# Contexts in sets of one quad, and one-bank pieces in a ring of four for the maximum pass

## The chip, the cores and the metric

The kernel runs on one core of one Trainium2 chip. The metric is the device time of one execution in microseconds (us). Five engines work side by side, each through its own list of instructions in order: TensorE (PE, matrix products), VectorE (DVE), ScalarE (ACT), GpSimd (POOL), and SyncE (SP), which here issues most of the DMAs. They wait for each other through semaphores. PE writes its results to PSUM, eight banks of 128 partitions by 512 fp32 columns; DVE and ACT read them from there.

## The reference

Two layers on 2048 tokens of width 128. Layer 0 is a Mamba block and then an attention block with a mixture of 16 experts; layer 1 is a second attention block and a mixture of 8 experts. The change touches only the two attention blocks. Each computes, for one sequence of 2048 tokens and 16 heads of width 8, in short:

```python
q, k, v = split(q), split(k), split(v)
...
scores = jnp.einsum("bhqd,bhkd->bhqk", q, k)
scores = jnp.where(causal, scores, neg)
attn = jax.nn.softmax(scores, axis=-1)
ctx = jnp.einsum("bhqk,bhkd->bhqd", attn, v)
...
```

The softmax needs the exact maximum of each query's row of scores before the exponentials are taken.

## The kernel before

Each head makes its scores twice. Queries and keys are cut into 16 tiles of 128 and four chunks of 512.

**The maximum pass** (`ring_piece` on PE, `ring_read` on DVE). PE multiplies a tile of 128 queries by up to 512 keys into `psum_b` (L840), DVE reduces the result to one maximum for each query (L1038 with the causal mask, which is a custom instruction followed by a short read of its accumulator; L1041 without a mask). The products are grouped into pieces by `MAX_PIECES`. Before the change a piece fills two banks (up to 1024 columns), there are 19 of them for a head, and `psum_b` is a ring of `NB = 2` such pieces: PE may start piece n when DVE has released piece n - 2. A head has 40 products in this pass and 24 reads. When the last piece of a head has been read, DVE runs five short instructions (L1046 to L1050), which split the negated maxima in three bf16 parts; PE transposes them (L844, the "maxrow", itself a ring piece), DVE copies them out (L1052), and SP sends them through memory into the rows of the queries' operand, so that the second pass gives scores with the maximum taken off.

**The second pass** (`scores`, `exp_piece`). PE makes the scores again, now keys by queries, into three banks of `psum_a` used in turn (L852; a diagonal block gets a product with the mask behind it, L855). ACT takes the exponential (L980) into a tile in SBUF. A head has 36 such steps ("slots"): for chunk c of the queries three for the diagonal quad of blocks and four for each full quad before it, c of them. Scores run three slots ahead of the slot in hand (`LOOK = 3`).

**The contexts** (`context`, `read_context`). For each quad, four fp32 products with 32 stationary columns each, in four column groups of the array, add to the fourth bank of `psum_a` (L870). The trace records each of the four as two. `SETS` says which quads go together: six sets for a head, four of them of two quads and two of one. A set stands in PE's order behind the scores of the slot in which its last quad's exponentials are awaited. When the last set of a chunk is done, ACT copies the bank out (L971). There is only one context bank, so the first set of the next chunk, the one with its diagonal quad, waits for that copy.

**The order.** `step_order` writes out what PE issues for a head: for each of the 36 slots the scores, then ring pieces until the DVE time they stand for has caught up with the slot, then a context set. `AHEAD_MAX` pieces of the head after the next are already made in this head, the rest of the next head's first. Heads go in pairs: once a pair, in its first head, PE also sums the two heads' contexts (L878, read by DVE at L1058) and transposes them (L885, read at L1063 and L1066); both use ring pieces. Before the first head stands a prologue (`FIRST_RING`) with the maxima alone, 29 pieces before the change. The last pair has no head behind it: its first head has only the rest of the last head's maxima to make, its second head none.

Of the kernel before, what the change touches and what calls it, by code (L numbers as in the profile page):

```python
# [12 lines left out]
P = 128  # L13
# [3 lines left out]
CW = 512  # L17
NC = T // CW
# [19 lines left out]
def program(nc, a, out):  # L38

    with ExitStack() as ctx:  # L40
# [10 lines left out]
        extra = sb("extra", [P, 4112])  # L51
        psum_a = ctx.enter_context(nc.psum_tensor("psum_a", [P, T], F32))
        psum_b = ctx.enter_context(nc.psum_tensor("psum_b", [P, T], F32))
# [485 lines left out]
        for c in range(NC):  # L539
            for ks in ((0,), (1,), (2, 3)):  # L540
                SCORES.append((c, [(4 * c + k, k, CW - k * P, (k - ks[0]) * 2 * P) for k in ks], "diagonal", c))
            for f in range(c):
# [5 lines left out]

        SETS = [(0, [("diagonal", 0)]), (1, [("diagonal", 1), ("full", 0)]), (2, [("diagonal", 2), ("full", 1)]), (2, [("full", 2)]),
                (3, [("diagonal", 3), ("full", 3)]), (3, [("full", 4), ("full", 5)])]  # L550
        NS_H = len(SETS)
        SET_OF = {q: n for n, (_, quads) in enumerate(SETS) for q in quads}
# [5 lines left out]
        def tail(i):  # L558
            return (i % 4 + 1) * P
        MAX_PIECES = [([(0, 0, P, 0), (2, 0, 3 * P, P), (3, 0, CW, CW)], [(0, 0, 0, P, True), (2, 0, P, 3 * P, True), (3, 0, CW, CW, True)]),  # L560
                      ([(1, 0, 2 * P, 0), (9, 2, 2 * P, 2 * P), (11, 2, CW, CW)],
                       [(1, 0, 0, 2 * P, True), (9, 1, 2 * P, 2 * P, True), (11, 1, CW, CW, True)]),
                      ([(8, 2, P, 0), (10, 2, 3 * P, P)], [(8, 1, 0, P, True), (10, 1, P, 3 * P, True)])]
        MAX_PIECES += [([(i, 0, CW, 0), (i, 1, tail(i), CW)], [(i, 0, 0, CW + tail(i), True)]) for i in range(4, 8)]
        MAX_PIECES += [([(i, 0, CW, 0), (i, 1, CW, CW)], [(i, 0, 0, 2 * CW, False)]) for i in range(8, 16)]
        MAX_PIECES += [([(i, 2, CW, 0), (i, 3, tail(i), CW)], [(i, 1, 0, CW + tail(i), True)]) for i in range(12, 16)]
        NB = 2
        NMAX = len(MAX_PIECES)
        AHEAD_MAX = 9
        SUM_SLOT, TURN_SLOT = 8, 14  # L570
# [71 lines left out]
        def attention(L, x_in, norm, w_cols, wt_raw):  # L642
            s = Attention()
# [42 lines left out]
            s.unread = extra[:, 1024:2048].bitcast(BF16).rearrange("p (b n) -> p b n", b=NB)  # L686
            s.mpart = extra[:, 2048:2080].rearrange("p (t c) -> p t c", c=2)
            s.mneg = extra[:, 2112:2128]
# [10 lines left out]
        def ring(n):  # L699
            return psum_b[:, (n % NB) * 2 * CW:(n % NB + 1) * 2 * CW]  # L700
        context_bank = psum_a[:, 3 * CW:4 * CW]
# [1017 lines left out]
```

How the kernel before makes its waits and increments, by code:

```python
        def turn_normed(e, name, xn, filled):  # L114
            for c in range(NC):
                e.wait_ge(tile_normed, normed(name) - NC + c + 1)
                for t in range(4 * c, 4 * c + 4):
                    i = e.transpose(psum_a[:, t * P:(t + 1) * P], xn[:, t * P:(t + 1) * P], ident[:, :])
                i.then_inc(filled, 1)
# [1 line left out]
        def read_turned(e, xT, filled, read):  # L122
            for c in range(NC):
                e.wait_ge(filled, c + 1)
                e.activation(xT[:, c * CW:(c + 1) * CW], psum_a[:, c * CW:(c + 1) * CW], ACT.Copy).then_inc(read, 1)
# [3 lines left out]
        def dve_link(e, ins):  # L130
            counts["dve"] += 1
            ins.then_inc(dve_step, 1)
            e.wait_ge(dve_step, counts["dve"])
# [1 line left out]
        def act_link(e, ins):  # L135
            counts["act"] += 1
            ins.then_inc(act_step, 1)
            e.wait_ge(act_step, counts["act"])
# [1 line left out]
        def pool_link(e, ins):  # L140
            counts["pool"] += 1
            ins.then_inc(pool_step, 1)
            e.wait_ge(pool_step, counts["pool"])
# [1 line left out]
        def norm_dve(e, name, src, dst, affine=None):  # L145
# [4 lines left out]
                    e.bn_stats(stats[:, bass.ds(4 * c + k, 1), :].rearrange("p a b -> p (a b)"),  # L150
                               src[:, ds(4 * c + k, D)]).then_inc(tile_stats, 1)
            e.wait_ge(tile_stats, NT * (n + 1))
            for t in range(NT):
# [127 lines left out]
        def mamba_pool(e):  # L281
            e.wait_ge(consts_ready, CONSTS)
            e.memset(xm[:, :, 0:3], 0.0).then_inc(xm_padded, 1)
```

## Time and profile before

| | |
|---|---|
| median of 3 runs | 2043.42 us (2042.29 to 2044.32) |
| profiled execution | 2041.5 us, span 2039.8 us |
| PE busy | 1564.7 us (77% of the span) |
| DVE busy | 1237.7 us (61%) |
| ACT busy | 875.0 us (43%) |
| first attention, first maximum product to last context | about 470 to 988 us |
| second attention | about 1277 to 1800 us |

The profile page gives busy time for each engine and the costliest groups of instructions. A busy PE is not a PE at its peak, since the ends of matmuls are modelled; starts are measured, so the distance from one start to the next is what counts for PE. The granted clock of PE is shown in tenths of full speed; 0.5 is its lower level.

### The profile page before, as it was taken

How to read it: one execution, taken by the hardware profiler on the slowest of the kernel's cores; microseconds unless marked ns; L12 is line 12 of the kernel's file. 1: busy time of each engine (PE TensorE's matmuls, PEld its weight loads, DVE VectorE, ACT ScalarE, POOL GpSimd, SP SyncE). 2: the span in 40 equal slices, each digit the busy share in tenths (PEclk: the TensorE clock that was granted, in tenths of full speed). 3: DMA queues.
4: the chain of work that ended last, by engine and by line, in shares of the span. 5: the costliest groups of instructions: out<-in, count | busy, mean ns of one | idle time of the engine just before them, and what ended most of it. 6: DMA issues, size and time to landing. Idle time of an engine off the chain costs nothing.

```text
span 2039.8 us, 27036 instructions
## 1 busy us (share of the span) xinstructions
PE 1564.7 (77%) x8103; PEld 671.6 (33%) x8104; DVE 1237.7 (61%) x2336; ACT 875.0 (43%) x1663; POOL 411.2 (20%) x267
## 2 busy tenths in 40 slices
PE   4817756636999999999524912799999999868999
PEld 2302222321333333332213802233333333235665
DVE  2479999476777777774240115777777777324444
ACT  2353323010766667666301301166666666631111
POOL 4019989110000011010123061001001110000000
PEclk9958889965999999998757956599999999968999
DMA  2002213013111111110141122211111110000000
GB/s 69 6 29 81 82 62 114 0 51 91 36 37 48 34 37 47 36 35 13 52 132 49 50 49 93 49 37 36 48 36 35 47 45 26 13 16 8 23 15 29
DMA packets 59071, 91.76 MB, mean 45 GB/s; under 512 B 13001, under 2 KB 39057, under 8 KB 58993
## 3 DMA queue, kind: packets, MB, share of 16 engines
q1 hardware_dynamic: 56962, 86.79, 14.7%
q0 software_dynamic: 2048, 4.20, 0.9%
q8 instruction: 33, 0.54, 0.1%
q14 instruction: 28, 0.23, 0.0%
HBM read 74.63 MB, written 16.32 MB: 45 GB/s over the span
## 4 chain that ended last, share of the span: by engine, by line
PE 59%; DVE 23%; issue 6%; ACT 5%; POOL 3%; DMA 2%; DVEq 1%; SPq 1%; POOLq 0%; ACTq 0%
PE psum_a L870 16%; PE psum_b L840 11%; PE psum_a L852 9%; DVE arena L516 5%; DVE extra L1038 5%; DVE arena L490 3%; PE psum_a L1509 3%; PE psum_b L1509 3%; PE psum_b L326 2%; DVE extra L1041 2%; PE psum_a L326 2%; PE psum_b L1518 2%; ACT psum_a L432 2%; PE psum_a L1518 1%; POOL expert_inputs L1259 1%
## 5 line engine op out<-in xcount | busy, mean ns | idle before, releaser
L980 ACT ACTIVATE arena<-psum_a 128x512 f32<-128x512 f32 (+3 forms) x1280 | 585.6, 546 | 254.5 <-PE psum_a L852 152.5
L1038 DVE CUSTOM_DVE_ANT_0 extra<-psum_b,mask_q 128x128 bf16<-128x128 f32 (+7 forms) x512 | 365.4, 755 | 200.5 <-PE psum_b L840 200.2
L840 PE MATMUL psum_b<-arena 72*128 72x512 bf16 (+3 forms) x1280 | 362.3, 372 | 94.1 <-DMA arena<-k_parts 50.8
L852 PE MATMUL psum_a<-arena 75*128 75x512 bf16 (+3 forms) x1280 | 395.2, 357 | 11.4 <-ACT arena L980 4.5
L1041 DVE TENSOR_REDUCE extra<-psum_b 128x1 f32<-128x1024 f32 x256 | 300.6, 1219 | 64.0 <-PE psum_b L840 62.6
L870 PE MATMUL psum_a<-arena,extra 128*32 128x512 f32 x2560 | 336.6, 637 | 2.2 <-ACT arena L980 2.2
L852 PEld LDWEIGHTS psum_a<-arena 75*128 75x128 bf16 x1280 | 118.3, 98 | 337.9 <-ACT arena L980 156.7
L295 POOL TENSOR_TENSOR arena<-arena,extra 128x1024 f32<-128x1024 f32 x48 | 170.9, 3574 | 130.0 <-DVE arena L516 118.0
L840 PEld LDWEIGHTS psum_b<-arena 72*128 72x128 bf16 x1280 | 102.0, 100 | 241.4 <-DVE extra L1038 108.1
L786 POOL TENSOR_TENSOR arena<-arena 128x512 f32<-128x512 f32 x64 | 81.1, 1268 | 465.1 <-ACT arena L971 310.5
L971 ACT ACTIVATE arena<-psum_a 128x512 f32<-128x512 f32 x128 | 76.4, 597 | 137.5 <-PE psum_a L870 137.5
L364 PE MATMUL psum_b<-arena,ident 128*128 128x512 f32 x192 | 104.1, 675 | 16.3 <-DVE arena L500 11.0
L870 PEld LDWEIGHTS psum_a<-arena,extra 128*32 128x32 f32 x2560 | 66.0, 112 | 135.4 <-issue 116.4
L774 POOL COPY extra<-arena 128x128 f32 (+1 forms) x32 | 9.5, 301 | 491.7 <-PE psum_a L870 491.7
L855 PE MATMUL psum_a<-mask_k,ident_bf 128*128 128x128 bf16 x512 | 100.2, 223 | 0.0
L354 PE MATMUL psum_a<-arena,select 96*128 96x512 bf16 x64 | 21.8, 425 | 98.0 <-DVE arena L490 93.3
L432 ACT ACTIVATE psum_a<-arena,a_neg 128x1024 f32<-128x1024 f32 x32 | 35.8, 1117 | 117.8 <-DVE arena L516 112.1
L490 DVE TENSOR_TENSOR arena<-arena,psum_a 128x2048 f32<-128x2048 f32 x32 | 72.4, 2263 | 1.5 <-PE psum_a L354 1.5
L1509 PE MATMUL psum_a<-arena 128*128 128x512 f32 x144 | 66.3, 604 | 6.8 <-DVE arena L1598 6.8
L174 ACT ACTIVATE spread<-spread 128x16 f32<-128x16 f32 x6 | 1.3, 216 | 149.7 <-DVE spread L156 149.7
L1509 PE MATMUL psum_b<-arena 128*128 128x512 f32 x144 | 64.8, 592 | 0.0
L1058 DVE COPY arena<-psum_b 128x512 f32<-128x512 f32 x16 | 11.1, 692 | 84.7 <-PE psum_b L878 83.0
(263 smaller groups left out, 1707.8 us busy)
## 6 DMA issues: line engine op xcount, KB each, us to landing
arena<-q_parts SPq DMA_DIRECT2D x192, 96.0 KB
arena<-k_parts SPq DMA_DIRECT2D x192, 96.0 KB
extra<-c_rows SPq DMA_DIRECT2D x32, 512.0 KB, 3.6
arena<-in_L_ffn_fc_w_dram SPq DMA_DIRECT2D x32, 256.0 KB, 5.9
k_parts<-arena SPq DMA_DIRECT2D x10, 512.0 KB, 5.6
q_parts<-arena SPq DMA_DIRECT2D x6, 512.0 KB, 5.0
arena<-in_L_ffn_w_dram SPq DMA_DIRECT2D x24, 128.0 KB, 2.1
expert_inputs<-zeros SPq DMA_DIRECT2D x4, 512.0 KB, 6.0
```

The costliest lines, as they stand in the source:

```text
L295: e.tensor_tensor(hc[step % 2][m], hs[step % 2][:, m, :], c_rows[step % NCB], ALU.mult).then_inc((hc0_done, hc1_done)[m], 1)
L364: i = e.matmul(psum_b[:, m * HALF + c * CW:m * HALF + (c + 1) * CW], ident[:, :], hc[step % 2][m][:, c * CW:(c + 1) * CW], start=(step % N ...
L490: e.tensor_tensor(dBu[step % 2], du[:, :, h * HALF:(h + 1) * HALF], psum_a[:, 0:HALF].unsqueeze(1).to_broadcast([P, NM, HALF]), ALU.mult). ...
L516: e.tensor_tensor_scan(hs[step % 2][:, m, :], (dA0, dA1[step % 2])[m], dBu[step % 2][:, m, :], start, ALU.mult, ALU.add).then_inc(scan_don ...
L840: m = e.matmul(ps[:, at:at + width], s.mq[0:ROWS, b, i * P:(i + 1) * P], s.mk[0:ROWS, b, c * CW:c * CW + width], start=True, stop=True)
L852: m = e.matmul(score_bank(p)[:, at:at + width], s.ek[0:ROWS + 3, b, j * P:(j + 1) * P], s.eq[0:ROWS + 3, b, (c + 1) * CW - width:(c + 1) * ...
L855: m = e.matmul(score_bank(p)[:, at:at + P], ident_bf[:, :], mask_k[:, :], start=False, stop=True)
L870: m = e.matmul(context_bank[32 * k:32 * k + 32, :], s.vs[:, b, j, :], probabilities(s, b, kind, quad, k, CW), start=(kind == "diagonal"), ...
L980: m = e.activation(probabilities(s, b, kind, quad, k, width), score_bank(p)[:, at:at + width], ACT.Exp)
L1038: m = e.tensor_tensor_reduce(s.unread[:, n % NB, at:at + length], ps[:, at:at + length], mask_q[:, 2 * CW - length:], 1.0, NEG, ALU.add, A ...
L1041: m = e.tensor_reduce(s.mpart[:, i, c:c + 1], ps[:, at:at + length], AX.X, ALU.max)
L1509: i = e.matmul(ps[:, (KH * m + k) * CW:(KH * m + k + 1) * CW], w[:, b, k * P:(k + 1) * P], xfT[:, c * CW:(c + 1) * CW], start=True, stop=True)
```

## The change

`SETS` becomes one set for each quad, ten for a head. Ring pieces become one bank wide: `max_piece` packs narrow products to 512 columns, a head has 34 pieces, `NB` is 4, so that PE may start piece n when piece n - 4 is released, and `AHEAD_MAX` is 17. The products of the maximum pass and their columns stay the same (40 products, 17408 columns for a head); the reads on DVE go from 24 to 40, 16 of them masked as before. `mpart` gets four columns for each tile in place of two. The rest follows from `step_order`.

```diff
--- before.py
+++ after.py
@@ -546,8 +546,9 @@
         LOOK = 3
         assert NSC % LOOK == 0
 
-        SETS = [(0, [("diagonal", 0)]), (1, [("diagonal", 1), ("full", 0)]), (2, [("diagonal", 2), ("full", 1)]), (2, [("full", 2)]),
-                (3, [("diagonal", 3), ("full", 3)]), (3, [("full", 4), ("full", 5)])]
+        SETS = []
+        for c in range(NC):
+            SETS += [(c, [("diagonal", c)])] + [(c, [("full", c * (c - 1) // 2 + f)]) for f in range(c)]
         NS_H = len(SETS)
         SET_OF = {q: n for n, (_, quads) in enumerate(SETS) for q in quads}
         SET_END = [max(p for p, x in enumerate(SCORES) if x[2:] in quads) for _, quads in SETS]
@@ -557,16 +558,21 @@
 
         def tail(i):
             return (i % 4 + 1) * P
-        MAX_PIECES = [([(0, 0, P, 0), (2, 0, 3 * P, P), (3, 0, CW, CW)], [(0, 0, 0, P, True), (2, 0, P, 3 * P, True), (3, 0, CW, CW, True)]),
-                      ([(1, 0, 2 * P, 0), (9, 2, 2 * P, 2 * P), (11, 2, CW, CW)],
-                       [(1, 0, 0, 2 * P, True), (9, 1, 2 * P, 2 * P, True), (11, 1, CW, CW, True)]),
-                      ([(8, 2, P, 0), (10, 2, 3 * P, P)], [(8, 1, 0, P, True), (10, 1, P, 3 * P, True)])]
-        MAX_PIECES += [([(i, 0, CW, 0), (i, 1, tail(i), CW)], [(i, 0, 0, CW + tail(i), True)]) for i in range(4, 8)]
-        MAX_PIECES += [([(i, 0, CW, 0), (i, 1, CW, CW)], [(i, 0, 0, 2 * CW, False)]) for i in range(8, 16)]
-        MAX_PIECES += [([(i, 2, CW, 0), (i, 3, tail(i), CW)], [(i, 1, 0, CW + tail(i), True)]) for i in range(12, 16)]
-        NB = 2
+        def max_piece(*reads):
+            at, products, taken = 0, [], []
+            for i, c in reads:
+                width = CW if c < i // 4 else tail(i)
+                products.append((i, c, width, at))
+                taken.append((i, c, at, width, c == i // 4))
+                at += width
+            return products, taken
+        MAX_PIECES = [max_piece((1, 0), (5, 1)), max_piece((9, 2), (13, 3))]
+        for g in range(NC):
+            MAX_PIECES += [max_piece((4 * g, g), (4 * g + 2, g)), max_piece((4 * g + 3, g))]
+            MAX_PIECES += [max_piece((i, c)) for i in range(4 * g, 4 * g + 4) for c in range(g)]
+        NB = 4
         NMAX = len(MAX_PIECES)
-        AHEAD_MAX = 9
+        AHEAD_MAX = 17
         SUM_SLOT, TURN_SLOT = 8, 14
 
         def step_order(first=False, turns=False, maxima=True, early=True, scores=True):
@@ -684,7 +690,7 @@
             s.oe_sum = slot(2).rearrange("p (c n) -> p c n", c=NC)
             s.sum_turned = slot(3)[:, 0:CW]
             s.unread = extra[:, 1024:2048].bitcast(BF16).rearrange("p (b n) -> p b n", b=NB)
-            s.mpart = extra[:, 2048:2080].rearrange("p (t c) -> p t c", c=2)
+            s.mpart = extra[:, 2048:2112].rearrange("p (t c) -> p t c", c=NC)
             s.mneg = extra[:, 2112:2128]
             s.mrest = extra[:, 2128:2144]
             s.mparts = extra[:, 2320:2384].bitcast(BF16)
@@ -697,7 +703,7 @@
             return s
 
         def ring(n):
-            return psum_b[:, (n % NB) * 2 * CW:(n % NB + 1) * 2 * CW]
+            return psum_b[:, n % NB * CW:(n % NB + 1) * CW]
         context_bank = psum_a[:, 3 * CW:4 * CW]
 
         def score_bank(p):
```

PE's order in the middle of chunk 3 (the last 512 queries) of a head, before. L870 is a context set (x4 is one quad, x8 are two), L852 a product of scores, L840 a product of the maximum pass.

```order
L870 MATMUL psum_a<-arena,extra 32x512 x8
L852 MATMUL psum_a<-arena 128x512
L840 MATMUL psum_b<-arena 128x512
L840 MATMUL psum_b<-arena 128x384
L852 MATMUL psum_a<-arena 128x512 x2
L840 MATMUL psum_b<-arena 128x512 x2
```

The same place after the change, where L876, L858 and L846 are the same three lines:

```order
L876 MATMUL psum_a<-arena,extra 32x512 x4
L858 MATMUL psum_a<-arena 128x512
L846 MATMUL psum_b<-arena 128x512
L846 MATMUL psum_b<-arena 128x128
L846 MATMUL psum_b<-arena 128x384
L858 MATMUL psum_a<-arena 128x512 x2
L846 MATMUL psum_b<-arena 128x512
L858 MATMUL psum_a<-arena 128x512
L846 MATMUL psum_b<-arena 128x512
L876 MATMUL psum_a<-arena,extra 32x512 x4
```

The context sets of two quads are gone. Four slots of scores and some four ring pieces of 512 columns now stand between two sets of one quad.

The second place is the maxrow in PE's order, before. L844 is its transpose; the pieces of 256, 256 and 512 columns and of 128 and 384 are the second and third of the head after the next.

```order
L870 MATMUL psum_a<-arena,extra 32x512 x4
L852 MATMUL psum_a<-arena 128x512
L840 MATMUL psum_b<-arena 128x256 x2
L840 MATMUL psum_b<-arena 128x512
L852 MATMUL psum_a<-arena 128x512 x3
L844 MATMUL psum_b<-ident_bf,extra 128x128
L840 MATMUL psum_b<-arena 128x128
L840 MATMUL psum_b<-arena 128x384
```

After the change (L850 is the maxrow, L861 the mask product; the last piece of the head's own maxima stands in the slot before the context set that begins these rows):

```order
L876 MATMUL psum_a<-arena,extra 32x512 x4
L858 MATMUL psum_a<-arena 128x512 x2
L861 MATMUL psum_a<-mask_k,ident_bf 128x128
L846 MATMUL psum_b<-arena 128x256 x2
L858 MATMUL psum_a<-arena 128x384
L861 MATMUL psum_a<-mask_k,ident_bf 128x128
L846 MATMUL psum_b<-arena 128x256 x2
L858 MATMUL psum_a<-arena 128x256
L861 MATMUL psum_a<-mask_k,ident_bf 128x128
L858 MATMUL psum_a<-arena 128x128
L861 MATMUL psum_a<-mask_k,ident_bf 128x128
L850 MATMUL psum_b<-ident_bf,extra 128x128
```

The maxrow stands four slots earlier, in the diagonal slots of chunk 3, and fewer products stand between the last piece and it.

## Rows read from the trace of the kernel before

**Rows 1.** Windows: prologue, a pair of heads, last head. Columns stand in the first line.

```profile
core 0: us, PE busy (x) PEld busy (x) DVE busy (x) ACT busy (x) POOL busy (x), PEclk, DMA share, GB/s
466.00:500.00 34.00, 22.54 (x55) 4.20 (x55) 26.45 (x65) 1.28 (x1) 2.75 (x3) 0.50 0.23 52
708.00:769.00 61.00, 58.18 (x366) 20.11 (x366) 44.79 (x97) 40.45 (x89) 5.63 (x6) 0.97 0.16 40
961.00:988.00 27.00, 22.74 (x140) 5.88 (x132) 0.00 (x0) 18.80 (x42) 3.79 (x3) 0.94 0.00 1
```

**Rows 2.** Timeline of PE, two maxrows ten heads apart: start, duration, engine, line, operation.

```profile
585.27 0.22 PE L844 MATMUL psum_b<-ident_bf,extra 128*128 128x128 bf16 x1
...
889.31 0.22 PE L844 MATMUL psum_b<-ident_bf,extra 128*128 128x128 bf16 x1
```

**Rows 3.** Timeline of PE, 685 to 691 us: two context sets, then plain products.

```profile
685.07 0.22 PE L855 MATMUL psum_a<-mask_k,ident_bf 128*128 128x128 bf16 x1
685.22 1.92 PE L870 MATMUL psum_a<-arena,extra 128*32 128x512 f32 x16
687.08 0.39 PE L852 MATMUL psum_a<-arena 75*128 75x512 bf16 x1
...
688.68 0.22 PE L855 MATMUL psum_a<-mask_k,ident_bf 128*128 128x128 bf16 x1
688.83 1.06 PE L870 MATMUL psum_a<-arena,extra 128*32 128x512 f32 x8
689.83 0.39 PE L852 MATMUL psum_a<-arena 75*128 75x512 bf16 x1
690.06 0.60 PE L840 MATMUL psum_b<-arena 72*128 72x512 bf16 x2
690.49 0.60 PE L852 MATMUL psum_a<-arena 75*128 75x512 bf16 x2
690.93 0.60 PE L840 MATMUL psum_b<-arena 72*128 72x512 bf16 x2
```

**Rows 4.** Timeline of PE and its weight loads: ring waits (idle time, releaser in brackets).

```profile
683.25 0.11 PEld L840 LDWEIGHTS psum_b<-arena 72*128 72x128 bf16 x2 [0.27 <-DVE extra L1038]
...
735.97 0.22 PE L844 MATMUL psum_b<-ident_bf,extra 128*128 128x128 bf16 x1
...
736.93 0.39 PE L840 MATMUL psum_b<-arena 72*128 72x128 bf16 x2 [0.74 <-DVE extra L1038]
```

**Rows 5.** Timeline of PE, a context set at the lower clock.

```profile
677.63 3.58 PE L870 MATMUL psum_a<-arena,extra 128*32 128x512 f32 x16
```

**Rows 6.** Timeline of DVE, masked reads one behind another, then unmasked ones.

```profile
471.28 0.29 DVE L1038 CUSTOM_DVE_ANT_0 extra<-psum_b,mask_q 128x128 bf16<-128x128 f32 x1 [14.17 <-PE psum_b L840]
...
471.50 0.55 DVE L1038 CUSTOM_DVE_ANT_0 extra<-psum_b,mask_q 128x384 bf16<-128x384 f32 x1
...
471.98 0.69 DVE L1038 CUSTOM_DVE_ANT_0 extra<-psum_b,mask_q 128x512 bf16<-128x512 f32 x1
...
472.59 0.42 DVE L1038 CUSTOM_DVE_ANT_0 extra<-psum_b,mask_q 128x256 bf16<-128x256 f32 x1
...
690.69 3.49 DVE L1041 TENSOR_REDUCE extra<-psum_b 128x1 f32<-128x1024 f32 x3 [0.34 <-PE psum_b L840]
```

**Rows 7.** Timeline of DVE: the five short instructions, then sum and turn.

```profile
493.24 0.18 DVE L1046 TENSOR_REDUCE extra<-extra 128x16 f32<-128x32 f32 x1
...
494.25 0.29 DVE L1038 CUSTOM_DVE_ANT_0 extra<-psum_b,mask_q 128x128 bf16<-128x128 f32 x1
...
694.31 0.69 DVE L1058 COPY arena<-psum_b 128x512 f32<-128x512 f32 x1
...
700.68 0.35 DVE L1063 RECIPROCAL extra<-psum_b 128x32 f32<-128x32 f32 x1
...
701.61 1.22 DVE L1038 CUSTOM_DVE_ANT_0 extra<-psum_b,mask_q 128x1024 bf16<-128x1024 f32 x1
```

**Rows 8.** Timeline of ACT: a context copy, then six exponentials in a row.

```profile
687.31 0.60 ACT L971 ACTIVATE arena<-psum_a 128x512 f32<-128x512 f32 x1 [1.43 <-PE psum_a L870]
...
690.55 2.94 ACT L980 ACTIVATE arena<-psum_a 128x512 f32<-128x512 f32 x6
```

## Prediction, written before the changed kernel ran

> **What bounds the kernel now.** I read the page's slices first, then windows, then the timeline of PE. Both attentions together fill about 1040 of the 2040 us. In the middle of one, PE is busy for 58.18 of 61 us, DVE for 44.79, ACT for 40.45 [rows 1]. A busy PE is not a full PE, so the question is how much of a head is work that PE must do. The maxrow comes once a head: from the one at 585.27 to the one ten heads later at 889.31 are 304.0 us, 30.4 us for a head [rows 2].
>
> PE's own work for a head, from distances between starts [rows 3]:
> - Four products of 512 columns take 690.93 - 690.06 = 0.87 us, 0.217 each. A head has 17408 columns in each pass, 68 times 512: 68 x 0.217 = 14.8 us.
> - 16 mask products of 128 columns: about 0.055 each, 0.9 us.
> - A context set of one quad: from the last mask product before it, which takes 0.055, to the next product, 689.83 - 688.68 - 0.055 = 1.10 us. A set of two: 687.08 - 685.07 - 0.055 = 1.96. The second quad adds 0.86, so that each set carries 0.24 beside its quads, half before its first product and half behind its last. Four sets of two and two of one: 4 x 1.96 + 2 x 1.10 = 10.0 us.
> - Sum (like a set of one, 1.1) and turn (0.3) once a pair, and the maxrow: 0.8 a head.
>
> That is 26.5 us. The other 3.9 us of 30.4 are waits and a lower clock. Three kinds show in rows. Behind the maxrow PE wants ring piece n + 1 and DVE has not yet released n - 1: from 735.97 to 736.93, 0.9 us beyond the maxrow's own 0.06 [rows 4]. Elsewhere in a burst of scores and pieces it waits shorter: a weight load sat idle for 0.27 us behind DVE at 683.25 [rows 4], and there are some ten such places a head (DVE mostly, ACT's three score banks in a few). And in some heads, right after these waits, the clock is at its lower level: a set of two quads takes 3.58 us at 677.63 against 1.92 at 685.22 [rows 3, 5]; the pair's mean clock is 0.97 [rows 1].
>
> DVE is not short of time, only late. Its reads back to back take 0.22, 0.34, 0.48 and 0.61 us for 128, 256 (between its neighbours), 384 and 512 masked columns, 1.043 ns a column and some 0.08 beside; three unmasked reads of 1024 take 3.49 us in all with 1.22 for the last, 1.14 each [rows 6]. A piece of two banks holds DVE for 1.14 us while PE fills one in 0.43, and with a ring of two PE may be only one piece ahead of the one being read. A context set of two then takes 1.96 us, in which DVE runs dry.
>
> **The change part by part.**
>
> *Ten context sets in place of six.* The eight products in two sets of one cost 2.20 in place of 1.96. Four more sets a head: 4 x 0.24 = 0.97 us, all on PE, nothing beside it hides it. For 32 heads 31 us. The row of a set of one stands in this very kernel, so I take it as it is.
>
> The Trainium skill, TensorEngine Tiling (Array Packing), section Tiling Modes, says that changing the tiling mode drains the array. A context set runs in four column groups and scores in none, so the rule speaks against this change. The 0.24 us of [rows 3] agree with it. The page gives no price, and the sum goes by the row.
>
> *Reads of one bank.* Unmasked, 8 of 1024 become 24 of 512. The trace has no unmasked read of 512; from above 0.61 (the masked one), from below half of 1.14 = 0.57. By the slope it is 1.14 - 0.53 = 0.60, which I take. Masked, two each of eight widths (128 to 1024) become four each of 128 to 512. DVE before: 8 x 1.14 + 2 x (0.22 + 0.34 + 0.48 + 0.61 + 0.75 + 0.88 + 1.01 + 1.15) = 20.0 us (the last four by the slope). After: 24 x 0.60 + 4 x (0.22 + 0.34 + 0.48 + 0.61) = 21.0. With the five short instructions (494.25 - 493.24 = 1.0), the maxrow's copy 0.2, and 0.69 + 0.93 once a pair for sum and turn [rows 7], DVE has 23.0 us a head. The extra 1.0 us costs nothing as long as PE needs more: its work is now 26.5 + 0.97 = 27.5 us.
>
> *What becomes of the waits for the ring.* Now each stretch between two sets has to be looked at, not the sum. In a full quad PE makes four scores and four pieces, 8 x 0.217 = 1.74, then a set, 1.10: 2.84 us. DVE gets 4 x 0.60 = 2.4. At the end of the burst it is 0.7 us behind, about one piece, and PE may be three ahead; in the set it catches up. In the diagonal slots PE has 1.6 + 1.10 against 2.3 to 2.6. Going through the ten stretches of a head, the only one with more DVE work than PE work is the one that holds the five short instructions (3.0 against 2.6), and it starts empty. So the ring's short waits go. Before, two quads together asked of DVE four to five pieces of 1.14 in a burst of 3.3 us: that is where they came from.
>
> *The maxrow.* The piece behind it now needs the release of the head's last piece, which comes before the five instructions: no wait. But the maxrow itself must find them done. From the end of the last piece's product DVE needs 0.2 to start, 0.5 that it is behind after three pieces in a row, 0.60 and 1.0: 2.4 us with the way back. PE has between them: scores 0.22, a set 1.10, 0.22, 0.27, a piece 0.22, 0.22, a piece 0.22, 0.27, in all 2.7. It fits. In the first head of a pair DVE also reads the turn just before (0.93, less 0.3 that PE itself spends): 3.0 against 2.7, a wait of 0.3. So 0.9 becomes 0.15 on average.
>
> *ACT.* It has 0.48 us an exponential (2.94 for six, the last taking 0.6 [rows 8]), 19 us a head, in bursts of four with a set behind them: 1.9 against 2.84. A score needs the exponential three slots back. With a piece in nearly every slot this way takes 1.3 us on PE, about what one score, its exponential and the two handovers take; I leave 0.1. SP's loads for the next head wait on contexts and on the maxrow, which both come no later; POOL's adds have 1.27 us of work a chunk and 27 us for four.
>
> *The clock.* The lower level comes in after the idle stretch at the maxrow; with it gone, I expect little of it: 0.1 a head.
>
> Sum for a head in the steady state: 27.5 + 0.15 + 0.1 + 0.1 = 27.8 us, 2.6 less than 30.4. This holds for 14 heads in each attention: 28 x 2.6 = 73 us. The last two heads of each have few or no pieces. The very last takes 27 us with PE busy for 22.74 and ACT for 18.80 [rows 1]; a score there waits for the exponential three back, 1.25 us against 0.65 of PE work, in every stretch, and this stays; what changes is that a set no longer leaves ACT dry for 1.96 us and that behind the last exponential stands one quad, not two. I take 2 us for each of these four heads, after their 0.97: 8 us. The prologue is DVE's: 26.45 busy of 34 us at the lower clock [rows 1]. It has 62 reads in place of 38 and 768 more columns, 24 x 0.07 + 0.8 = 2.5 us more, against waits that go in about the same amount: 0.
>
> The sum against the profiled execution's 2041.5 us: - 73 - 8 = 1960.5. The median of the runs is 1.9 us above that execution, so the forecast is 1962 us.
>
> **The rivals.**
>
> *A. Half of the waits stay.* Each piece has its own handover, 34 a head in place of 19. If a handover costs 0.07 us more on DVE than the back-to-back reads show, DVE has 25.4 us against 27.5 and is late in each stretch with 3 or 4 pieces; then some 1.5 us a head of waits remain. For it: register work for each wait stands in the loop, and DVE is already short in the stretch with the maxrow. Against: reads that follow one another across pieces show none of it [rows 6]. Gain 1.1 x 32 = 35 us: 2008. The skill's VectorE: DVE Perf Modes, in its section on the TRN2 errata, has a read from PSUM cost 120 cycles beside its columns (125 ns). The rows show 70 to 80 ns back to back; by the page's figure DVE would have some 2 us more a head and this rival would be the likelier one. The measured distances decide.
>
> *B. Slower: the one context bank.* The first set of chunks 1 to 3 waits for ACT's copy of the bank. Before, the set behind a chunk's last was seven or more slots off; now it is three. After the set PE has five or six products of 0.217, 1.1 to 1.3 us. ACT started a copy 0.24 us after a set's end and took 0.60 [rows 3, 8]: 0.84, a margin of 0.25. But ACT reaches the copy only after the three exponentials issued before the set (1.4 us); the set gives it 1.0. If it is a further exponential late, the copy ends 1.3 us later, PE stands, ACT then runs dry, and the waits feed each other: three places x 1.3 = 3.9 us a head against the 3.6 of waits and clock that go. With the 0.97: 1.3 x 32 = 41 us slower, 2084. It decides from about 1.2 us a place on; below it the change still gains.
>
> *C. More.* No wait at all, and the last heads near ACT's 19 us: 27.5 a head, 4 us for each last one: 1940.
>
> **How the numbers follow.** The forecast (1945 to 1985) 0.62; A (1985 to 2030) 0.22; B 0.08; C 0.08. The predicted time is 1962. The range reaches down to C and over most of A: 1938 to 2020, which leaves out B and A's tail. A time within 0.2% (4 us) is about what cannot be told from no change; between A and B little falls there. Faster 0.91, same 0.02, slower 0.07.
>
> **What would show it.** Distance between maxrows near 27.8 us. A set of one quad still at 1.10 us, with ten of them a head. PE's wait for DVE behind the maxrow gone, a short one before it in every other head. The unmasked read of 512 columns at 0.60 us from start to start. The window's mean clock at 1.00. It would be wrong if PE waited for ACT's copy before the sets of chunks 1 to 3 (B), if waits for DVE before pieces stayed in the hundreds of ns (A), or if the lower clock came anyway.

## The result, and the profile after

| | before | after |
|---|---|---|
| median (4 runs each, same chip) | 2043.12 us (2042.29 to 2044.32) | 1947.29 us (1946.09 to 1948.78) |
| ratio | | 0.9531 [0.9514, 0.9547] |
| profiled span | 2039.8 us | 1944.3 us |
| start of first score of head 0 to that of head 14, both attentions | 421.0 + 427.7 us | 387.7 + 387.4 us |
| head 14 (the first of the last pair), from first score to first score | 34.0, 30.9 us | 27.9, 27.9 us |
| last head, start of first score to start of last context product | 27.5, 28.2 us | 23.4, 23.4 us |
| first maximum product to first score | 34.0, 34.3 us | 32.2, 32.3 us |

The kernel is 4.7% faster. Of the 95.5 us of span, 73.5 went in heads 0 to 13, 18.0 in the last two heads of each attention and 3.7 in the two prologues. Some 25 us of this is what the lower clock level cost the kernel before in places where the changed kernel has the full clock; the part on the prediction works it out.

The page after. The first line is busy time of each engine, the other a group of instructions, the unmasked reads (busy us, mean ns of one | idle us before them, and what ended most of it):

```profile
PE 1526.5 (79%) x8103; PEld 660.5 (34%) x8104; DVE 1270.9 (65%) x2848; ACT 884.0 (45%) x1663; POOL 411.3 (21%) x267
...
L1047 DVE TENSOR_REDUCE extra<-psum_b 128x1 f32<-128x512 f32 x768 | 486.6, 683 | 71.8 <-PE psum_b L846 70.0
```

Windows of after, the answer to [rows 1]: prologue, heads 1 to 13, a pair, last head. The columns are those of [rows 1].

```profile
466.00:500.00 34.00, 26.83 (x59) 5.64 (x59) 28.08 (x86) 1.28 (x1) 3.04 (x3) 0.50 0.28 65
532.00:890.00 358.00, 358.00 (x2370) 125.42 (x2367) 304.77 (x830) 267.32 (x572) 38.01 (x40) 1.00 0.15 42
708.00:769.00 61.00, 61.00 (x401) 20.99 (x398) 52.04 (x138) 45.36 (x96) 6.92 (x7) 1.00 0.14 40
918.00:942.00 24.00, 21.79 (x149) 5.97 (x145) 0.00 (x0) 21.02 (x46) 3.83 (x3) 1.00 0.00 1
```

The same stretch of heads before (533 to 925 us), and what PE waited for in it by the waits view (total us, times, longest):

```profile
533.00:925.00 392.00, 373.19 (x2375) 129.95 (x2374) 291.21 (x623) 263.73 (x573) 37.83 (x40) 0.98 0.15 39
...
PE psum_b L840 <- DVE extra L1038: 10.6, 19, 0.7
PE psum_b L878 <- DVE extra L1041: 2.3, 6, 0.4
PE psum_b L885 <- DVE extra L1038: 1.3, 6, 0.2
```

For after, the waits view of 532 to 890 us is empty for PE, and PE is busy for all 358 us. The modelled ends hide short gaps, so the view gives only the waits that outlast them; starts show more. By starts (distance less the columns' own time) about 2.9 us of waits a head stood before, 0.9 of them right behind the maxrow and the rest at some ten other places. Now nothing above 0.1 us is left beside the sets' own boundaries, and some 0.5 us a head in handovers of 1 to 14 ns.

Two maxrows ten heads apart, the answer to [rows 2]. They give 276.82 / 10 = 27.68 us a head, where it was 30.40:

```profile
577.21 0.23 PE L850 MATMUL psum_b<-ident_bf,extra 128*128 128x128 bf16 x1
...
854.03 0.23 PE L850 MATMUL psum_b<-ident_bf,extra 128*128 128x128 bf16 x1
```

PE around a maxrow, and a set of one quad in the middle of a head (timeline; the answers to [rows 3, 4]):

```profile
695.91 0.38 PE L846 MATMUL psum_b<-arena 72*128 72x512 bf16 x1
696.22 1.06 PE L876 MATMUL psum_a<-arena,extra 128*32 128x512 f32 x8
697.22 0.39 PE L858 MATMUL psum_a<-arena 75*128 75x512 bf16 x1
...
714.77 0.22 PE L861 MATMUL psum_a<-mask_k,ident_bf 128*128 128x128 bf16 x1
714.82 0.22 PE L850 MATMUL psum_b<-ident_bf,extra 128*128 128x128 bf16 x1
714.88 0.38 PE L846 MATMUL psum_b<-arena 72*128 72x128 bf16 x2
715.19 1.06 PE L876 MATMUL psum_a<-arena,extra 128*32 128x512 f32 x8
```

The maxrow starts 0.05 us after the mask product, its own columns, and the piece behind it 0.06 later: both waits are gone. In the other head of a pair (577.21, above) it starts 0.09 us late. The set costs 697.22 - 695.91 - 0.217 = 1.10 us from product to product: 0.10 ahead of it, 0.86 in it, 0.145 behind it, and the same for all ten sets of a head.

DVE in the stretch with the five short instructions, and two context copies of ACT, the first in the last head and the second in a steady one (the answers to [rows 6 to 8]):

```profile
711.39 1.88 DVE L1047 TENSOR_REDUCE extra<-psum_b 128x1 f32<-128x512 f32 x3 [0.53 <-PE psum_b L846]
713.31 0.22 DVE L1052 TENSOR_REDUCE extra<-extra 128x16 f32<-128x64 f32 x1
...
714.19 0.18 DVE L1056 TENSOR_TENSOR extra<-extra 128x16 bf16<-128x16 f32 x1
714.45 0.43 DVE L1044 CUSTOM_DVE_ANT_0 extra<-psum_b,mask_q 128x256 bf16<-128x256 f32 x1
```

```profile
927.13 0.60 ACT L977 ACTIVATE arena<-psum_a 128x512 f32<-128x512 f32 x1 [0.26 <-PE psum_a L876]
...
589.69 0.60 ACT L977 ACTIVATE arena<-psum_a 128x512 f32<-128x512 f32 x1 [0.77 <-PE psum_a L876]
```

Before its three reads in a row DVE sat idle for 0.53 us and waited for PE: DVE now runs dry, where PE was late before. The reads back to back start 0.60 us apart (0.597 to 0.607). In heads 1 to 13 the copies end 0.37 to 1.03 us before the next chunk's first set. In the last head it is closer: the copy from 922.79 ends at 923.39, three scores end their columns at 922.66 + 3 x 0.217 = 923.31, and the set starts at 923.53, 0.12 later than the 0.10 ahead of every set.

```profile
922.79 0.60 ACT L977 ACTIVATE arena<-psum_a 128x512 f32<-128x512 f32 x1
...
922.66 0.82 PE L858 MATMUL psum_a<-arena 75*128 75x512 bf16 x3
923.53 1.07 PE L876 MATMUL psum_a<-arena,extra 128*32 128x512 f32 x8
```

### The profile page after: what moved, and what is told of

Its sections match the earlier page's. It is cut to its first block, busy times and chain, and to the rows that moved or that the text cites. A ratio compares the mean times of both kernels' runs of the same rounds, so it can differ in the third digit from the quotient of the medians.

```text
span 1944.3 us, 28236 instructions
## 1 busy us (share of the span) xinstructions
PE 1526.5 (79%) x8103; PEld 660.5 (34%) x8104; DVE 1270.9 (65%) x2848; ACT 884.0 (45%) x1663; POOL 411.3 (21%) x267
## 4 chain that ended last, share of the span: by engine, by line
PE 67%; DVE 20%; ACT 4%; POOL 4%; issue 3%; DMA 2%; SPq 1%; DVEq 1%; POOLq 0%; ACTq 0%
PE psum_a L876 17%; PE psum_a L858 14%; PE psum_b L846 11%; DVE arena L516 5%; DVE arena L490 4%; PE psum_a L1515 3%; PE psum_b L1515 3%; PE psum_b L326 2%; PE psum_a L326 2%; PE psum_b L1524 2%; ACT psum_a L432 2%; PE psum_a L1524 2%; POOL expert_inputs L1265 2%; DVE extra L1047 2%; POOL arena L1271 2%
## 5 line engine op out<-in xcount | busy, mean ns | idle before, releaser
L986 ACT ACTIVATE arena<-psum_a 128x512 f32<-128x512 f32 (+3 forms) x1280 | 594.8, 537 | 194.0 <-PE psum_a L858 103.2
L1047 DVE TENSOR_REDUCE extra<-psum_b 128x1 f32<-128x512 f32 x768 | 486.6, 683 | 71.8 <-PE psum_b L846 70.0
L846 PE MATMUL psum_b<-arena 72*128 72x512 bf16 (+3 forms) x1280 | 422.9, 368 | 53.2 <-DMA arena<-k_parts 51.5
L858 PE MATMUL psum_a<-arena 75*128 75x512 bf16 (+3 forms) x1280 | 415.5, 353 | 3.7 <-ACT arena L986 3.7
L876 PE MATMUL psum_a<-arena,extra 128*32 128x512 f32 x2560 | 342.7, 607 | 1.8 <-ACT arena L986 1.4
L1044 DVE CUSTOM_DVE_ANT_0 extra<-psum_b,mask_q 128x512 bf16<-128x512 f32 (+3 forms) x512 | 224.5, 486 | 78.1 <-PE psum_b L846 65.3
L858 PEld LDWEIGHTS psum_a<-arena 75*128 75x128 bf16 x1280 | 118.5, 98 | 350.8 <-ACT arena L986 287.2
L846 PEld LDWEIGHTS psum_b<-arena 72*128 72x128 bf16 x1280 | 118.8, 100 | 172.3 <-DMA arena<-k_parts 51.8
L861 PE MATMUL psum_a<-mask_k,ident_bf 128*128 128x128 bf16 x512 | 100.7, 223 | 0.0
L876 PEld LDWEIGHTS psum_a<-arena,extra 128*32 128x32 f32 x2560 | 50.7, 108 | 110.3 <-ACT arena L986 51.2
L861 PEld LDWEIGHTS psum_a<-mask_k,ident_bf 128*128 128x128 bf16 x512 | 51.0, 100 | 32.2 <-issue 1.6
```

The lines of the kernel that those rows point to most:

```text
L846: m = e.matmul(ps[:, at:at + width], s.mq[0:ROWS, b, i * P:(i + 1) * P], s.mk[0:ROWS, b, c * CW:c * CW + width], start=True, stop=True)
L858: m = e.matmul(score_bank(p)[:, at:at + width], s.ek[0:ROWS + 3, b, j * P:(j + 1) * P], s.eq[0:ROWS + 3, b, (c + 1) * CW - width:(c + 1) * ...
L861: m = e.matmul(score_bank(p)[:, at:at + P], ident_bf[:, :], mask_k[:, :], start=False, stop=True)
L876: m = e.matmul(context_bank[32 * k:32 * k + 32, :], s.vs[:, b, j, :], probabilities(s, b, kind, quad, k, CW), start=(kind == "diagonal"), ...
L986: m = e.activation(probabilities(s, b, kind, quad, k, width), score_bank(p)[:, at:at + width], ACT.Exp)
L1044: m = e.tensor_tensor_reduce(s.unread[:, n % NB, at:at + length], ps[:, at:at + length], mask_q[:, 2 * CW - length:], 1.0, NEG, ALU.add, A ...
```

## The experiments

Ratios are to the kernel before on the same chip, whose median went from 2036.5 to 2043.1 us between chips, so ratios, spans and heads are compared and not medians. "A head" is the mean over heads 3 to 12 of the first attention, five pairs, by the starts of first scores. Outside the attentions the profiled runs differ for no reason that the edits give: the stretch between the two took 283.7 to 291.0 us and the one behind the second 238.5 to 244.0; in the changed kernel, profiled twice, they took 290.6 and 290.4, and 240.8 and 244.0. Differences of a few us in the total are therefore no verdict, those in a head are.

**1. Sets alone.** The kernel before with ten sets of one quad; pieces stay two banks wide, `NB = 2`.

```diff
-        SETS = [(0, [("diagonal", 0)]), (1, [("diagonal", 1), ("full", 0)]), (2, [("diagonal", 2), ("full", 1)]), (2, [("full", 2)]),
-                (3, [("diagonal", 3), ("full", 3)]), (3, [("full", 4), ("full", 5)])]
+        SETS = []
+        for c in range(NC):
+            SETS += [(c, [("diagonal", c)])] + [(c, [("full", c * (c - 1) // 2 + f)]) for f in range(c)]
```

> The kernel before with ten context sets of one quad for a head and nothing else: pieces stay two banks wide in a ring of two. Theory (the ring gives the gain, the splitting of sets costs 0.24 us of PE for each set more, but its short bursts also let two-bank pieces through): PE's own work rises from 26.5 to 27.5 us a head; in a stretch of four slots there are two pieces of 1.14 us for 2.84 us of PE, so most waits in the bursts go, but the one behind the maxrow (0.9 us) and the lower clock after it stay: about 29.2 us a head, 30.4 before, some 2000 us in all. Rival (the splitting gives the whole gain, the ring is idle trim): 27.7 us a head as in the changed kernel, 1950 us. Second rival (splitting only costs, the ring does all): 30.4 + 0.97 = 31.4 us a head, 2074 us.

Measured: 1980.34 us, 0.9724 [0.9702, 0.9745]; 28.49 us a head, where I had expected 29.2, last heads 23.4. PE's window and waits in heads 1 to 13:

```profile
533.00:902.00 369.00, 362.11 (x2374) 123.36 (x2373) 294.99 (x622) 268.25 (x572) 38.00 (x40) 1.00 0.15 42
...
PE psum_b L841 <- DVE extra L1039: 6.8, 18, 0.7
```

The four extra boundaries cost 0.97 us a head, and still the head is 1.9 shorter, some 0.7 of it because no lower clock came in heads 1 to 13: shorter bursts alone take away more than half of the waits (by starts 0.9 us a head are left of 2.9). What stays is 0.38 us a head behind the maxrow, where I had left 0.9, and 0.86 once a pair behind the turn.

**2. Ring alone.** The changed kernel with the six old sets.

> The changed kernel with the six context sets of before (four of them two quads): one-bank pieces in a ring of four stay. Theory: PE's own work is 26.5 us a head. In a stretch of seven or eight slots PE makes its scores and pieces in 3.5 us, DVE reads them in 4.8, so it is 1.3 us or two pieces behind before the set, and the ring allows three: no waits for the ring. ACT has 8 x 0.48 = 3.8 us for 3.5, which its three banks take up. So 26.8 to 27.3 us a head, 0.4 to 0.9 less than the changed kernel's 27.7, and 1920 to 1935 us: the splitting of the sets is a loss there. Rival (the set of two, 1.96 us, is what makes PE wait, through ACT and DVE running dry and bursting): 28.5 to 29.5 us a head, 1975 to 2005 us.

Measured: 1952.91 us, 0.9588 [0.9572, 0.9604]; 27.59 us a head; heads 14 take 30.3 and 30.7, last heads 27.7 and 26.7. The first three rows are in a steady head, the others in the last one:

```profile
592.71 0.38 PE L845 MATMUL psum_b<-arena 72*128 72x512 bf16 x1
593.10 0.39 PE L857 MATMUL psum_a<-arena 75*128 75x512 bf16 x1
593.10 0.10 PEld L857 LDWEIGHTS psum_a<-arena 75*128 75x128 bf16 x1 [0.51 <-ACT arena L985]
...
937.32 1.86 PE L857 MATMUL psum_a<-arena 75*128 75x512 bf16 x4 [0.45 <-ACT arena L985]
...
944.00 0.88 PE L875 MATMUL psum_a<-arena,extra 128*32 128x512 f32 x4 [1.08 <-ACT arena L985]
```

I had expected 26.8 to 27.3, since four boundaries go. They do, but some 0.9 us of waits come back in their place: a score behind a set of two waits 593.10 - 592.71 - 0.217 = 0.17 us, and many slots of a burst of seven or eight about 0.05. The products that come late are scores, and their weight loads waited for ACT: a burst of eight is paced by ACT's three score banks. So with the ring of four the split of the sets is worth nothing in the steady state (27.68 against 27.59). It pays in the last two heads, 51.3 us against 57.4 and 58.0. Part of the latter is the lower clock, of which 2 had spells there; a last head without one takes 26.7 us in 2 against 23.4.

The two parts overlap: 2.8% and 4.1% alone, 4.7% together.

**3 and 4. A ring of three, a ring of two.** The changed kernel with fewer one-bank buffers.

```diff
-        NB = 4
+        NB = 3
```

> The changed kernel with a ring of three one-bank pieces in place of four (one bank left unused). Theory: PE may be two pieces ahead of the one being read, 1.2 us of DVE time; in most stretches DVE ends the burst 0.7 us behind, plus 0.2 us for the handover, so a few waits of 0.1 to 0.3 us come back, in the diagonal stretches and round the five short instructions most: 27.9 to 28.3 us a head, 1955 to 1968 us. Rival (it is the width of the pieces alone, not how many are in flight): 27.7 us a head, 1947 us.

> The changed kernel with a ring of two one-bank pieces (two banks unused). Theory: PE may be one piece ahead; in each burst it goes at DVE's pace, 0.60 us a piece and more where the handovers (0.2 us each way) show, so four slots take 2.4 us or more where they took 1.74, less one piece ahead: 0.3 to 0.6 us for each of ten stretches, 31 to 34 us a head, 2050 to 2140 us, slower than the kernel before. Rival (width alone): 27.7 us a head, 1947 us.

Measured, ring of three: 1969.97 us, 0.9674 [0.9653, 0.9695], 28.56 a head. Ring of two: 2096.99 us, 1.0294 [1.0276, 1.0311], 32.50 a head. Waits of PE, ring of three and then ring of two, over 13 heads each:

```profile
PE psum_b L846 <- DVE extra L1044: 5.4, 13, 0.6
PE psum_b L884 <- DVE extra L1047: 1.7, 6, 0.3
```

```profile
541.00:962.00 421.00, 388.06 (x2377) 126.21 (x2373) 309.24 (x830) 271.81 (x572) 37.95 (x40) 1.00 0.14 36
...
PE psum_b L846 <- DVE extra L1044: 8.9, 26, 0.5
PE psum_b L846 <- DVE extra L1047: 8.3, 26, 0.3
PE psum_b L850 <- DVE extra L1044: 5.7, 13, 0.5
```

With three, one wait a head comes back, right behind the maxrow (0.8 and 0.4 us in the two heads of a pair by starts), and one ahead of the sum: these are the places with the most DVE work at once. With two, PE waits everywhere, the L1047 rows among them. One-bank pieces in a ring of two are 2.9% slower than the kernel before. Against 1, which has the same ten sets and two pieces of two banks, the head goes from 28.49 to 32.50, and it has half of the banks too. So narrow pieces give nothing by themselves; what they do is to make a ring of four fit in the same four banks. Three was a little dearer than I thought (27.9 to 28.3), two came as expected (31 to 34).

**5 and 11. The sum beside a context set.** Twice the same kernel. In the changed kernel the sum (four column groups too) moves one slot on, right ahead of a set.

```diff
-        SUM_SLOT, TURN_SLOT = 8, 14
+        SUM_SLOT, TURN_SLOT = 9, 14
```

> The changed kernel with SUM_SLOT = 9 in place of 8: in the first head of each pair the sum (32 stationary columns in four column groups, like a context set) stands directly before the third context set instead of alone between scores. Theory (the 0.24 us of a set is the change from whole-array products to column-group products and back, 0.10 on the way in and 0.145 on the way out): sum and set pay it once, the distance from the sum to the set has no 0.145 and no 0.10, a pair is 0.24 us shorter (54.86 us for the two heads of a pair in place of 55.36 would be twice that, 55.12 is expected), 14 pairs: 3 to 4 us of 1947, a ratio about 0.002 lower than the changed kernel's. Rival (each group of eight records pays its own fill, whatever stands before it): no difference in a pair.

> The kernel with the sum beside a context set once more, on the same chip as the two with merged sets: 27.56 us a head, a ratio of 0.951 to the kernel before.

Measured: 1939.94 us, 0.9504 [0.9474, 0.9535], and again on another chip 1937.73 us, 0.9501 [0.9482, 0.9521]; 27.562 us a head against 27.681, in both runs. First the changed kernel (sum L884, later its set), then this one:

```profile
567.60 1.07 PE L884 MATMUL psum_b<-arena,sum_groups 128*32 128x512 f32 x8
568.60 0.28 PE L858 MATMUL psum_a<-arena 75*128 75x256 bf16 x1
...
569.20 1.06 PE L876 MATMUL psum_a<-arena,extra 128*32 128x512 f32 x8
570.20 0.39 PE L858 MATMUL psum_a<-arena 75*128 75x512 bf16 x1
```

```profile
567.66 1.07 PE L884 MATMUL psum_b<-arena,sum_groups 128*32 128x512 f32 x8
568.54 0.61 PE L876 MATMUL psum_a<-arena,extra 128*32 128x512 f32 x4
...
569.52 0.39 PE L858 MATMUL psum_a<-arena 75*128 75x512 bf16 x1
```

Sum and set take 1.00 us each apart and 569.52 - 567.66 = 1.86 together, and the gap of 0.10 ahead of one of them goes as well: 0.24 once a pair, 0.12 a head. The price is that of a change and not of a set. Sets and sum are fp32 and the products around them bf16, so the type could be what counts; the turn, fp32 too but over the whole array, says no:

```profile
573.27 0.38 PE L846 MATMUL psum_b<-arena 72*128 72x512 bf16 x1
573.49 0.60 PE L891 MATMUL psum_b<-ident,arena 128*128 128x128 f32 x4
573.93 0.38 PE L858 MATMUL psum_a<-arena 75*128 75x512 bf16 x1
```

It starts 0.22 us after a bf16 product, that product's own columns, and its four transposes take 0.44 us up to the next bf16 product, four times the 0.11 from one to the next. So the price goes with the narrow products in column groups; what about them costs it, the runs do not tell further. This bears out the Trainium skill, TensorEngine Tiling (Array Packing), section Tiling Modes: it lays the drain on a change of mode and not on a change of tile.

**6 and 7. A fourth score bank**, taken from the ring (`LOOK = 4`, `NB = 3`, the maxrow one piece later), with ten sets and with the old six.

> The changed kernel with the eighth bank moved: four banks of scores (LOOK = 4), a ring of three one-bank pieces, maxrow one piece later in the order; ten context sets. Theory: in the changed kernel ACT holds PE up for nothing in the steady state, so the fourth score bank gives nothing there, and the ring of three costs some of the 0.87 us a head that it cost alone (most of that stood behind the maxrow, which now comes one piece later): 27.9 to 28.3 us a head; the last head of each attention, where PE waits for the exponential three slots back, gets shorter than 23.4 us, to 21 or 22. In all 1950 to 1965 us. Rival (the ring needs its fourth bank everywhere): 28.5 us a head, 1970 us.

> As the kernel with four score banks, but with the six context sets of before. Theory (in the kernel with six sets and a ring of four it was ACT, three banks deep, that gave the 0.97 us of the saved boundaries back as waits of 0.05 in each slot and 0.2 behind each set): with four score banks these waits go, PE's own work is 26.5 us a head, the ring of three costs 0.3 to 0.8: 26.8 to 27.4 us a head, 1925 to 1945 us, the fastest of all. Rival (ACT's pace of 0.48 us a slot against PE's 0.434 is what counts in a burst of eight slots, one more bank only puts it off): 27.5 us a head and more, 1950 us or slower.

Measured: with ten sets 1953.79 us, 0.9564 [0.9522, 0.9606], 28.09 a head, last head 20.9. With six 1974.07 us, 0.967 [0.9627, 0.9714], 28.58 a head, last head 24.8. The last head, where PE had waited for ACT, gets 2.5 us shorter with ten sets; the steady heads lose 0.4, since the bank is missed in the ring. With six sets I was wrong by over 1 us a head: I had counted on ACT's waits going, and waits for DVE took their place (a ring of three in bursts of eight slots: by starts 1.7 us a head, in pieces of 0.1 to 0.4). By the heads the bank is worth more in the ring; the totals of 6 and 8, on the same chip, do not tell the two apart.

**8. The changed kernel again**, beside 5 to 7 on their chip.

> The changed kernel once more, on the same chip as the other three, so that they can be compared with it: a ratio of 0.953 to the kernel before.

Measured: 1949.33 us, 0.955 [0.951, 0.959]; 27.681 a head, last head 23.4, as in its first run.

**9 and 10. Two sets merged, one set merged** into sets of two quads (diagonal 2 with full 1, and in 9 full 4 with full 5 too), both with the sum moved as in 5.

> The kernel with the sum beside a context set, and eight context sets in place of ten: the diagonal quad and the first full quad of chunk 2 together, and the last two quads of chunk 3 together. In the kernel with six sets and a ring of four, PE waited for ACT in the burst before the first of these 0.10 us and before the second 0.15 us, before the two others merged there 0.23 and 0.41. Theory (a merged set gives 0.24 us back and costs what ACT, paced at 0.48 us a slot, is then late): 0.48 - 0.25 = 0.23 us a head less than 27.56 in the steady state, 27.33; the last two heads, where ACT sets the pace, lose about 0.9 us for each merged set, 1.5 to 2.5 us an attention. In all 0 to 4 us faster than the kernel without the merging, within 0.2%. Rival (ACT's lateness depends on how many sets are merged in a head, not where): no gain in the steady state either, and 4 to 8 us slower in all.

> As before with nine sets: only the diagonal quad and the first full quad of chunk 2 together. Theory: 0.24 - 0.10 = 0.14 us a head less than 27.56, 27.42 in the steady state, 4 us in 28 heads, less 0.5 to 1 us for each last pair: 2 to 3 us faster than the kernel with ten sets. Rival: the same as ten sets, or slower.

Measured: 9: 1938.08 us, 0.95 [0.9479, 0.9522], 27.294 a head, last heads 27.0 and 26.6. 10: 1942.25 us, 0.953 [0.9509, 0.955], 27.373 a head, last heads 25.7 and 24.1. The steady heads do as expected, but the last ones give it back, 3.4 us each in 9 where I expected 1.5 to 2.5; spells of the lower clock from 914.4 and 1696.1 us on are part of it. The total of 10 should have been 2 to 3 us below that of 5 and is not. By the heads it gains 0.19 x 28 = 5.3 us and loses 3.0 in the last heads, and another 3 went with the lower clock, in head 0 of the first attention (30.7 us against 28.8 in 11) and head 14 of the second (28.9 against 27.7). Both attentions together take 875.6 us from first score to last context product, 875.1 in 11: whether one merged set gains is open.

**12. Merged in all heads but the last pair.** As 5, but two of a head's sets are issued a few slots later, together with the next one, in every head except those of the last pair.

```diff
-                    if SET_SLOT[n] == t:
+                    if SET_SLOT[n + 1 if early and n in (3, 8) else n] == t:
```

> The kernel with the sum beside a context set, in which the two sets that were merged before stand together again, in all heads but the last pair of each attention. Theory: 27.29 us a head in the steady state, as with two sets merged, and the last head at 23.4 us without a spell at the lower clock, as with ten sets. Against the kernel with ten sets 27.56 - 27.29 = 0.27 us for each of 28 heads, 7.5 us less in all: about 1930 us, a ratio of 0.946 to the kernel before, the fastest. Rival (the loss in the last pair has to do with what stands before it): no better than the kernel with two sets merged everywhere, 0.950.

Measured: 1932.04 us (1930.45 to 1938.59), 0.9482 [0.946, 0.9505]; 27.293 us a head, heads 14 28.6 (27.7 in 11), last heads 23.4. The shorter steady heads and the short last heads stand side by side, at 0.9 us more for each head 14; both attentions together take 867.0 us, 8.1 less than in 11. It has the lowest ratio of all and a span of 1928.7 us, against 1940.3 and 1937.7 in 5 and 11 and 1944.3 in the changed kernel; its interval still meets those of 5, 9 and 11.

## Why the prediction was right, and where it was off

The forecast was 1962 us, with 1945 to 1985 for its own case; 1947.3 came, near the lower end. Step by step:

- **PE's own work.** The set of one stayed at 1.10 us ([rows 3] and 695.91 to 697.22), and the four extra ones are paid in full. Forecast 27.5 us a head of PE work, and 27.68 came in all.
- **The ring's waits** went. The argument by stretches, PE work against reads between two sets, is borne out from three sides: shorter bursts alone remove over half of the waits (1), depth alone nearly all of DVE's (2; 0.09 us before the sum is left), and one buffer less brings back just the stretch with the most DVE work (3).
- **The maxrow.** Forecast 0.3 us in one head of a pair and none in the other; 0.09 and 0 came, and no wait behind it.
- **DVE.** Reads of 512 at 0.60 us as interpolated. Rival A rested on a dearer handover of each piece; the run of three takes 713.31 - 711.39 = 1.92 us, with the handover to the next instruction in it. The Trainium skill's VectorE: DVE Perf Modes (section on the TRN2 errata) has 125 ns beside the columns of such a read; back to back these rows show 0.60 - 512 x 0.001043 = 0.07, so the measurement decides against the page here.
- **Rival B**, the copy of the one context bank, had the right place and nearly the right margin (0.25 us said, 0.37 to 0.68 at the sets of chunks 1 to 3 of the steady heads), and did not decide there; it would take ACT nearly a further exponential late. In the last head the first set of each of the chunks 1 to 3 does wait for the copy, 0.12 to 0.13 us each (923.53, above), 0.4 us in a head.
- **Sum of the heads 0 to 13.** Forecast -73 us, measured -73.5. Some 20 us of it is the clock, read from the starts of first scores and the profile's granted clock. In heads 1 to 13 the kernel before had ten spells of 3.4 us at the lower level, four in the first attention and six in the second. A head with one takes 30.15 us where its like takes 28.5, or 32.64 for 30.98: 1.4 to 1.7 us each, 16 in all. Head 0 of the second attention, with 15.4 us at the lower level against 6.3 in the first, took 32.9 us against 28.9. At full clock a head of before takes (28.5 + 30.98) / 2 = 29.74 us, so the ring and the sets gave 2.06 us a head and not 2.7. The prediction had waits and clock in one sum of 3.9 us; that the clock's part came too, for a reason that the runs do not bear out (below), was luck as far as they show.

Two terms were mis-sized and are most of the 15 us. **The last two heads** of each attention: forecast -2 us each, -8 in all; they gave -18.0. Of this 5.4 us is again the clock, which that term left out: in the last pairs the kernel before had spells of 10.2, 3.4 and 3.4 us and the changed kernel none. The first cost 34.02 - 30.93 = 3.1 us, the other two 0.8 and 1.5 (without them both last heads take 26.7 us, like the one without a spell in 2). The other 12.6 us are 3.0 for each head 14 and 3.3 for each last head. I had said that the wait for the exponential three back stays in every stretch, some 0.6 us each. It does not with short sets:

```profile
928.87 0.82 PE L858 MATMUL psum_a<-arena 75*128 75x512 bf16 x3
929.95 0.39 PE L858 MATMUL psum_a<-arena 75*128 75x512 bf16 x1 [0.26 <-ACT arena L986]
930.27 1.07 PE L876 MATMUL psum_a<-arena,extra 128*32 128x512 f32 x8
...
941.48 1.06 PE L876 MATMUL psum_a<-arena,extra 128*32 128x512 f32 x8 [0.69 <-ACT arena L986]
```

In the view a stretch of four full slots waits 0.26 us, the diagonal stretches 0.19 in three of four, and a stretch of three full slots not at all. A burst of seven or eight waits 0.45 first, before and in 2. By starts the waits of the last head fell from 6.9 to 3.5 us; with one quad in place of two behind the last wait (0.86) and the four boundaries (0.97) that makes the 3.3. The wait for the last exponential is 0.69 us now and was 1.08, before and in 2; in 2 the two quads behind it stand at a granted clock of 0.55:

```profile
944.00:946.50 2.50, 2.50 (x16) 0.59 (x16) 0.00 (x0) 0.00 (x0) 0.00 (x0) 0.55 0.00 0
```

ACT's busy time in the last head says the same: 21.02 of 24 us, where it was 18.80 of 27 [rows 1]. Here ACT is the bound, and I had not worked these stretches out one by one as I did the steady ones. **The prologue** gave -3.7 us in two, forecast 0. From first maximum product to first score DVE was busy for 31.0 us where it had been 30.2, 0.8 more and not the 2.5 that I had costed, and its idle time went from 3.8 to 1.3 us. The remaining 0.3 us are outside the attentions.

**The clock** was right in size and not in its reason. The window's granted clock is 1.00 in heads 1 to 13, where the kernel before has spells like the one of which the first row below tells. I had written that the lower level comes in after the idle stretch at the maxrow. The ring of two speaks against it: its PE waits more at the same place (1.1 to 1.3 us around the maxrow by starts, against 0.8 to 0.9), is busy for 388.06 of 421 us, and shows 1.00 in all of them. The kernel before, at 373.19 of 392, had four spells of 3.4 us in that stretch. So the share of idle time and the wait at the maxrow do not by themselves bring the lower level. What does is open; no experiment was aimed at it alone. In the last pairs such a spell came in the kernel before and in 1, 2, 3, 5, 6, 7, 9 and 10, in some of them in one attention only, but not in the changed kernel (twice), 4, 11 and 12. 5 and 11 are the same kernel: head 14 of the second attention took 29.1 us with a spell in 5 and 27.7 without one in 11 (the second row and the third). So a spell can come or not with nothing changed, and neither the size of the sets nor the ring's depth sorts the runs there.

```profile
616.00:620.00 4.00, 3.92 (x19) 0.72 (x19) 1.73 (x6) 0.88 (x2) 0.00 (x0) 0.57 0.46 117
...
1660.00:1672.00 12.00, 10.17 (x58) 2.41 (x54) 2.98 (x9) 7.48 (x17) 0.00 (x0) 0.86 0.01 2
...
1660.00:1672.00 12.00, 10.38 (x66) 3.29 (x63) 6.80 (x17) 8.37 (x18) 0.00 (x0) 1.00 0.01 2
```

In the heads 1 to 13 no run but the kernel before has a spell in either attention.

## What to carry to other kernels

Compare producer and consumer stretch by stretch between the producer's other jobs, not over the loop: a ring must hold what the consumer is behind at the end of the longest burst, and either a deeper ring or shorter bursts will do that, so the gains of the two do not add up. Products in four column groups cost 0.24 us for each run of neighbours and not for each set, so put them side by side where there is slack. Heads at the end of a loop, with one kind of work missing, have another bound than the steady ones and may want another order; work them out apart. And before a saving is put down to a change, compare stretches at the same granted clock: here a quarter of it was the clock.

## What the runs showed of the hardware

- A change between full-width products and four column groups costs 0.10 us going in and 0.145 coming out at full clock, the same in all sets of heads 1 to 13, and nothing between two neighbours in column groups, even when they write different PSUM tensors (5). A change between bf16 and fp32 over the whole array costs nothing of the kind (573.27 to 573.93).
- The lower clock level came in spells of 3.4 us in heads 1 to 13 of the kernel before, whose PE idles for 5% of them, and not in those of the ring of two, which idle for 8%. Each cost a head 1.4 to 1.7 us. In the last pair a spell came in one run of a kernel and not in another run of the same (5 and 11).
- One quad of four fp32 products with 32 stationary and 512 moving columns each holds PE for 0.86 us, as long as four bf16 products of 512 columns.
